# Gathers of an MoE's second half waiting one pair further back, and one shared tile moved ahead of the routed ones

## What is computed

```python
def _L0_ffn_ref(x, gate_w, W1, b1, W2, b2, sW1, sb1, sW2, sb2):
    TOP_K = 2
    logits = x_flat @ gate_w.T
    probs = jax.nn.softmax(logits.astype(jnp.float32), axis=-1)
    top_w, sel = jax.lax.top_k(probs, TOP_K)
    top_w = top_w / jnp.sum(top_w, axis=-1, keepdims=True)
    ...
    h = jax.nn.gelu(jnp.einsum('th,ehf->tef', x_flat, W1) + b1[None], approximate=False)
    y = jnp.einsum('tef,efh->teh', h, W2) + b2[None]
    out = jnp.einsum('teh,te->th', y, combine)
    sh = jax.nn.gelu(x_flat @ sW1 + sb1, approximate=False)
    out = out + sh @ sW2 + sb2
x = x + jnp.tanh(g_xattn[0]) * _L0_xattn_ref(_layernorm(x), ctx_1024, ctx_1024, mask, ...)
x = x + jnp.tanh(g_ffn[0]) * _L0_ffn_ref(_layernorm(x), ...)
```

## Time and profile before

| | us |
|---|---|
| median of 3 runs | 576.25 |
| lowest and highest of them | 572.81, 577.24 |
| the profiled execution | 571.52 |
| its span, first to last instruction | 569.9 |
| mean TensorE clock granted, share of full | 0.961 |

### The profile page before, as it was taken

The page is one execution under the profiler, slowest core; times in us unless marked ns, Lnnn a source line. Parts: engine busy times, 40 slices in busy tenths (PEclk is TensorE's granted clock), DMA queues, the critical chain, the costliest instruction groups (busy, mean ns, idle before and its releaser), DMA issues.

```text
span 569.9 us, 12480 instructions
## 1 busy us (share of the span) xinstructions
PE 530.3 (93%) x3195; PEld 461.8 (81%) x3196; DVE 361.6 (63%) x787; ACT 243.2 (43%) x535; POOL 292.3 (51%) x267
## 2 busy tenths in 40 slices
PE   4788899998979799999999999999999999999996
PEld 3578798997978577888888888888888888888885
DVE  3357676767753488665555566565556565558887
ACT  2224576765653433334343443334334334433341
POOL 7137377898576587442444443444344450045550
PEclk9797899999886699999999999999999999999999
DMA  5863546666572234766756566566766641123352
GB/s 145 186 199 94 175 133 178 172 191 198 158 199 84 93 129 129 250 194 189 211 175 200 171 224 174 175 193 221 202 221 193 221 129 37 37 74 104 114 150 74
DMA packets 58266, 91.17 MB, mean 160 GB/s; under 512 B 6669, under 2 KB 43901, under 8 KB 58245
## 3 DMA queue, kind: packets, MB, share of 16 engines
q0 software_dynamic: 24800, 57.82, 34.8%
q1 hardware_dynamic: 24933, 25.70, 14.3%
q10 hardware_dynamic: 8512, 7.40, 4.3%
HBM read 68.15 MB, written 16.65 MB: 149 GB/s over the span
## 4 chain that ended last, share of the span: by engine, by line
PE 69%; POOL 10%; issue 10%; DVE 5%; DMA 1%; SPq 1%; ACT 1%; another core or an unknown queue 1%; ACTq 1%; POOLq 0%; DVEq 0%
PE ps L782 17%; PE ps L783 8%; PE ps L769 8%; PE ps L770 8%; PE ps L771 8%; PE ps L757 8%; POOL xn L462 3%; POOL x2row L479 2%; PE ps L750 2%; POOL xres L468 1%; PE ps L840 1%; PE ps L722 1%; DMA front<-in_ctx 1%; PE ps L826 1%
## 5 line engine op out<-in xcount | busy, mean ns | idle before, releaser
L782 PE MATMUL ps<-w2hl,hTh 128*128 (+1 forms) x440 | 160.0, 404 | 1.7 <-DVE hTl L1310 1.7
L783 PE MATMUL ps<-w2hl,hTl 128*128 (+1 forms) x440 | 122.4, 278 | 0.0
L1156 ACT ACTIVATE hid<-hid 128x512 f32<-128x512 f32 x110 | 69.0, 632 | 123.3 <-DVE hid L1316 121.8
L1150 ACT ACTIVATE hTh<-ps 128x512 fp32r<-128x512 f32 x110 | 60.6, 596 | 101.8 <-PE ps L757 89.7
L782 PEld LDWEIGHTS ps<-w2hl,hTh 128*128 128x128 f32 x440 | 82.6, 188 | 19.0 <-issue 2.1
L769 PE MATMUL ps<-w1l,xT 128*128 (+1 forms) x220 | 93.3, 424 | 1.4 <-issue 1.4
L1316 DVE TENSOR_TENSOR hid<-ps,b1bc 128x512 f32<-128x512 f32 x110 | 74.7, 688 | 25.5 <-PE ps L771 22.4
L770 PE MATMUL ps<-w1h,xT 128*128 (+1 forms) x220 | 87.9, 400 | 0.0
L771 PE MATMUL ps<-w1h,xT 128*128 (+1 forms) x220 | 87.7, 398 | 0.0
L783 PEld LDWEIGHTS ps<-w2hl,hTl 128*128 128x128 f32 x440 | 82.9, 188 | 0.0
L1310 DVE TENSOR_TENSOR hTl<-ps,hTh 128x512 fp32r<-128x512 f32 x110 | 71.3, 685 | 9.4 <-ACT hTh L1150 6.1
(11 more groups left out here) (194 smaller groups left out, 832.8 us busy)
## 6 DMA issues: line engine op xcount, KB each, us to landing
stage<-in_L_ffn_W POOLq DMA_DIRECT2D x14, 1024.0 KB, 5.5
w1h<-in_L_ffn_W POOLq DMA_DIRECT2D x7, 1024.0 KB, 6.0
w2hl<-in_L_ffn_W POOLq DMA_DIRECT2D x7, 1024.0 KB
qstack<-moved_q SPq DMA_DIRECT2D x48, 128.0 KB, 2.5
xrow<-routed_x SPq DMA_DIRECT2D x39, 128.0 KB
routed_y<-yrow ACTq DMA_DIRECT2D x39, 128.0 KB, 1.7
moved_q<-hid SPq DMA_DIRECT2D x16, 256.0 KB, 3.5
b1bc<-in_L_ffn_b POOLq DMA_DIRECT2D x8, 512.0 KB, 6.3
```

The costliest lines, as they stand in the source:

```text
L782: mm(p_y, hTh[:, c, :], part(2 * D), start=c == 0, stop=False)
L783: last = mm(p_y[:, 0:D], hTl[:, c, :], part(D), start=False, stop=c == FC - 1)
L1150: act.activation(hTh[:, n * (FC // 2):(n + 1) * (FC // 2), :], p_hT[:, n, :, :], ACT.Copy).then_inc(S["hT_hi"], 1)
L1156: act.activation(hid[:, n, :], hid[:, n, :], ACT.Gelu).then_inc(S["h_act"], 1)
```

## The change

NA goes from 6 to 7, so that token tile 6 runs ahead of the routed tiles, and NB from 10 to 9. The total stays 55 tiles. COMBINED has one entry less, and its 7th and 8th entries hold three token tiles instead of two. The first gather of a pair waits for the landing of the pair two in front instead of the one in front.

```diff
-    NA = 6
+    NA = 7
...
             for t in range(NT):
-                if t % 2 == 0 and t:
-                    pool.wait_ge(g_in[t // 2 - 1], 16 * 2 * TOP)
+                if t % 2 == 0 and t > 2:
+                    pool.wait_ge(g_in[t // 2 - 2], 16 * 2 * TOP)
...
-            COMBINED = ((), (), (0, 1), (2, 3), (4, 5), (6, 7), (8, 9), (10, 11), (12, 13), (14, 15))
+            COMBINED = ((), (), (0, 1), (2, 3), (4, 5), (6, 7), (8, 9, 10), (11, 12, 13), (14, 15))
```

## The result

The changed kernel takes 616.12 us, the median of 4 runs (609.0 to 620.14), and the kernel before, beside it, 576.75 us (4 runs, 572.81 to 578.12): a ratio of 1.0626, with a 95% interval of 1.0559 to 1.0693. The forecast was 577.4 us in a range of 573.0 to 581.5. It is missed by 38.7 us, and the result lies outside the range. The ratio leaves out runs over 1.5% above the fastest of the same kernel (here 619.5 and 620.14 us).

What follows compares the result with a forecast made beforehand. PE bounds the kernel; tiles 0, gathers 0, table +1.2 and signals 0 on the profiled 571.52 give 572.7 us, or 576.25 + 1.2 = 577.4 us for the median, in a range of 573.0 to 581.5.

Steps and rivals of the forecast that it cites:

- The gathers: POOL's stream: 32 gathers at 1.25 us, no wait for a landing, two or three out at once; 0 us.
- The seventh early tile: Moves one PE tile of 6.67 us from behind the routed tiles to ahead of them; 0 in the sum.
- What bounds the kernel: PE, busy 93% of the span; the change can gain only at three places where PE waits.
- rival C: Port rule: each gather is held for one more DVE instruction, 0.69 us; +9.4, 585.7 us; chance 0.02.
- the trace disagrees here: Said against the skill's port rule: all 32 gathers take 942 to 1067 ns with DVE mostly busy beside them.
- the table: Sixteen combinations in seven calls instead of eight make tile 53's result 0.8 or 1.7 us later; taken at 1.2 us.
- An unclear cost: signals that come late beside gathers: Late tiles: PE's signals seem held up while POOL issues gathers; one tile loses 0.94 us again, so 0 change.
- -0.94 and +4.7 as bounds: Late-signal cost: either the 0.94 us goes, or all six tiles beside the gathers lose 0.94 (+4.7).
- 12 us of POOL, which nobody waits for: The edit of the gathers' wait saves POOL some 12 us, which nobody waits for.
- A: The gather stream without pauses holds up PE's signals in every tile; +5.9, 582.1 us; chance 0.14.
- B: The pauses were the harm, or the gathers' earlier end frees the last calls; -1.0, 575.2 us; chance 0.17.

Runs made afterwards that it cites:

- experiment 8: The kernel before with its old wait and ten late tiles, but the denser combination table: 574.89 us, ratio 0.9975.
- Experiments 3 and 4: Changed kernel with gathers in bursts of eight, then a pause: 601.36 us; changed kernel with a 1.83 us memset on POOL between pairs: 581.0 us.
- experiment 5: The changed kernel with its 32 gathers replaced by plain DMAs from POOL, leaving out the permutation: 570.11 us (one run).
- experiment 6: The kernel before with the new wait and a 0.55 us memset on POOL behind each gather: 570.51 us, ratio 0.992.

## Why the prediction was wrong

Right:
- **The gathers.** A row at 1.25 us, without a wait for a landing, and eight never in flight; the earlier trace rows were enough for that. The last one starts 38.9 us after the first, as worked out (31 x 1.25 = 38.8). The first started 17.2 us later than before, not 6.7, as the other 10.5 us had been lost ahead of the gathers.
- **The seventh early tile, 0.** The new wait alone, with six, has the same late loss (36.2 and 36.3 us).
- **What bounds the kernel.** PE is busy 200.00 of 200.00 us from 300 to 500, as in the earlier trace rows. A loss could only come from PE being made to wait, and it did.
- **The port, rival C.** All 32 gathers take 942 to 1024 ns, as in the earlier trace rows, so no gather was held up behind DVE, and its price wasn't paid. The rule in the Trainium skill (SBUF — State Buffer, "Who interferes with whom") is for instructions in a two-port mode, and it says that `tensor_tensor` has none. From 503 to 558 us of the kernel before DVE runs 56 TENSOR_TENSOR and 32 SCALAR_TENSOR_TENSOR and nothing else. Rival C was priced with such an instruction, L1310. So the prediction's "the trace disagrees here" says too much: the rows settle rival C, and not the rule.

A term of the wrong size: **the table**, taken at 1.2 us between 0.8 and 1.7. It costs 0.6 to 0.7 (experiment 8). The six combinations take 2.83 us in one piece, as forecast (2.87). The forecast took the result of tile 53 to come 0.8 us later, or 1.7 if `tile(53)` passed its delay on. It comes 0.9 us after the last transposes (567.43 and 566.54 in experiment 8), against 0.2 before, so 0.7 later: no delay is passed on, and PE loses nothing at `tile(54)`'s first layer either.

The failed step: **"An unclear cost: signals that come late beside gathers"**, taken at 0, with -0.94 and +4.7 as bounds. I had seen the effect in the earlier trace rows and named its cause rightly: PE's signals are held up while POOL issues gathers. The price was wrong by 36 us, in two ways.
- I multiplied the 0.94 us of one tile by the number of tiles that would now stand beside the stream. That takes each tile's delay as its own. But in the earlier trace rows POOL paused for 2.09 us behind every fourth gather, and the regularity that I had noted (ACT's rows start about 1 us after the fourth gather has been issued) says that the delay ends in the pause. What the edit removes is the pause. Then nothing bounds the delay but the end of the stream: the signals come 2.0, 4.3, 8.7, 14.3 and at last 33.5 us late. Experiments 3 and 4 show it: bursts twice as long lose 25.4 us and not 2 x 0.94, and a pause of 1.83 us that waits for nothing brings the late part down from 100.6 to 66.8.
- I called the wait "12 us of POOL, which nobody waits for". For data that is so. But it was also what kept POOL's issuing at 0.56 of the time, and the table above turns between 0.57 and 0.65. The 2 us pauses looked like a cost, and were the cure.

Of the rivals, A had the mechanism and the sign, at 5.9 us instead of 38. B ("the pauses were the harm") was the reverse of the truth. The bound of +4.7 was no bound: it was worked out from rows in which the mechanism was cut short every 5 us, and for a stream without pauses the profile of before has no row. The honest upper end would have been that the delay runs as long as the stream, 39 us, since ACT's start at 543.14 was 2.4 us late already, half of the 5 us that POOL had issued in a row.

Of the 37.5 us the rest is the end, 2.2 us longer: 0.6 to 0.7 of it is the table. The other 1.5 is the clock: in the last call five of the second layer's L782, from 610.88 us on, take 0.63 us in place of 0.39, each step 0.64 in place of 0.35: the 1.2 GHz level, after PE had waited 1.99 us for DVE. PE had waited 2.00 us in experiment 8 as well, and 1.99 in experiment 5, and there every L782 behind the wait's first takes 0.39 or 0.40 us; in experiment 8 the last result comes 1.5 us sooner after the transposes. Why the clock fell in the one and not in the others isn't tried.

Three things stay open. What inside the chip holds up PE's signals, and in the end its instructions, isn't settled by these runs. They say only that PE is hit most and POOL a little, that it needs indirect DMAs issued by POOL, that bytes and landings don't matter, that the share of the time spent issuing does, and that it lasts some 5 us past the last issue. Whether the recording has a part in it isn't known: every run on record has a span and a granted clock of its own, so none shows the kernel unrecorded. And the trace of the changed kernel holds only 5 to 18 of each pair's 64 landing records (4 gathers of 16), that of experiment 5 all 64, so records are being lost beside the gathers. The third is the front of the second half (52.6 to 59.3 us for the first seven tiles). Its length doesn't go with what was changed; its differences make the medians differ by some us where the late parts agree to 0.1. So of experiment 6's gain of 0.8%, 1.0 us (63.16 to 62.14) is explained, the rest is not.

## What to carry to other kernels

A wait that nobody waits for may still pace a stream. Before it is loosened, look for rows whose releaser is remote, or which start late after work that is done, beside that stream: they say that it disturbs others already, and their size under the present pauses is no bound for the size without them. Indirect DMAs from POOL should be spread out (here one per 1.66 us lost nothing) while PE works in short exchanges with ACT and DVE; a memset on POOL, which had nothing else to do here, made a pause that cost nothing.

## What the runs showed of the hardware

- Indirect DMAs issued by POOL in a row at 1.25 us hold up what PE hands to ACT and DVE, by up to 33.5 us (the second layer's end at 532.55, DVE's start at 566.11), and later space PE's own matmuls 2.1 to 2.8 us apart. What ACT and DVE hand on comes through at once, as the gelu's end at 536.40 and PE's start at 536.46.
- Plain DMAs from POOL, 0.54 us each and issued for 0.9 of the time, in rows of at most 4.3 us, do nothing of the kind (every pitch 6.67 us). Gathers of half the bytes do as much as whole ones (36.1 and 36.3 us lost).
- It has a sharp onset: 0 to 1.8 us are lost at 0.56 or 0.57 of the time issuing, 22.9 and 25.4 at 0.65, 36 at 0.75.
- It outlasts its cause: the last issue ends at 560.63, and ACT and DVE get their signals at about 566.1. With that, PE's idle time took the granted clock to the 1.2 GHz level (0.50 from 540 to 560 us); from 580 to 600 us it is 1.00 again.
